# Row maxima over 1024 keys in pairs of PSUM banks in place of twice 512 in single banks

## What is computed

```python
qkv = x @ qkv_w.T + qkv_b                       # reshaped to 16 heads, hd = 8
scores = jnp.einsum('hbds,hbdt->hbst', q, k) / jnp.sqrt(jnp.float32(hd))
w = jax.nn.softmax(scores, axis=-1)             # over 1024 keys
attn = jnp.einsum('hbst,hbdt->hbsd', w, v)
return attn @ out_w.T + out_b
```

## Time and profile before

| | us |
|---|---|
| runs of the kernel | 629.66, 629.94, 626.11 |
| median | 629.66 |
| span of the profiled execution | 623.5 |
| that execution's own time | not shown |
| TensorE busy in the span | 546.7 |
| VectorE busy | 480.4 |
| ScalarE busy | 349.4 |
| mean granted TensorE clock, share of full speed | 0.929 |

### The profile page before, as it was taken

One profiled execution on the slowest core, in us unless ns is written; L12 is line 12 of the kernel. 1 busy time (PEld: TensorE's weight loads), 2 busy tenths in 40 slices (PEclk: granted clock), 3 DMA queues, 4 the chain that ended last, 5 costly groups with the idle time before them and its releaser, 6 DMA issues.

```text
span 623.5 us, 9634 instructions
## 1 busy us (share of the span) xinstructions
PE 546.7 (88%) x2831; PEld 218.8 (35%) x2831; DVE 480.4 (77%) x965; ACT 349.4 (56%) x667; POOL 113.0 (18%) x155
## 2 busy tenths in 40 slices
PE   2986899872591699999999999899999999999887
PEld 2443656561110133333333333233333333323366
DVE  6999579971593388888898898788888888863473
ACT  2764314433000377777777677677777777778551
POOL 6947708334000000100100100100100000000000
PEclk9997899887555599999999999999999999999999
DMA  8030000021221000010010010010010000000001
GB/s 205 8 69 0 2 1 1 5 82 74 87 85 81 25 1 2 27 52 2 29 51 2 29 51 2 32 51 2 19 61 2 2 2 1 1 2 1 1 18 52
DMA packets 14664, 18.95 MB, mean 30 GB/s; under 512 B 3801, under 2 KB 12936, under 8 KB 13448
## 3 DMA queue, kind: packets, MB, share of 16 engines
q1 hardware_dynamic: 13818, 17.54, 8.2%
q0 software_dynamic: 240, 0.46, 0.7%
q10 hardware_dynamic: 550, 0.27, 0.1%
HBM read 12.75 MB, written 4.19 MB: 27 GB/s over the span
## 4 chain that ended last, share of the span: by engine, by line
PE 69%; DVE 16%; DMA 8%; ACT 3%; issue 2%; SPq 2%; POOL 0%; ACTq 0%; DVEq 0%
PE ps L1256 20%; PE ps L1229 18%; PE ps L1294 17%; PE ps L1034 5%; PE ps L1044 5%; DVE mx L895 3%; DMA qt<-nm_s 3%; DVE acc L794 3%; DMA kt<-k_scr 2%; DVE h L710 2%; DVE acc L840 1%; DMA k_scr<-gate 1%; PE ps L1243 1%; ACT gate L648 1%; DVE st L687 1%
## 5 line engine op out<-in xcount | busy, mean ns | idle before, releaser
L895 DVE TENSOR_REDUCE mx<-ps 128x1 f32<-128x512 f32 x512 | 319.5, 681 | 70.8 <-PE ps L1229 70.8
L648 ACT ACTIVATE gate<-ps 128x512 f32<-128x512 f32 x256 | 134.3, 604 | 112.2 <-PE ps L1294 112.2
L1229 PE MATMUL ps<-kt,qt 72*128 72x512 bf16 x384 | 157.7, 417 | 18.0 <-DMA kt<-k_scr 18.0
L1294 PE MATMUL ps<-qt,kt 96*128 96x512 bf16 x384 | 143.0, 386 | 21.6 <-DMA qt<-nm_s 18.2
L648 ACT ACTIVATE acc<-ps 128x512 f32<-128x512 f32 x256 | 132.3, 602 | 49.8 <-PE ps L1294 49.8
L1229 PEld LDWEIGHTS ps<-kt,qt 72*128 72x128 bf16 x384 | 38.3, 100 | 131.9 <-DVE mx L895 81.0
L1256 PE MATMUL ps<-gate,v 128*32 128x512 f32 x512 | 69.3, 611 | 0.7 <-ACT o_sb L639 0.7
L1256 PE MATMUL ps<-acc,v 128*32 128x512 f32 x512 | 68.2, 605 | 0.6 <-ACT acc L648 0.6
L446 POOL CAST nm_s<-nm 16x128 bf16<-16x128 f32 x16 | 4.6, 287 | 331.4 <-DVE nm L908 331.4
L1294 PEld LDWEIGHTS ps<-qt,kt 96*128 96x128 bf16 x384 | 37.5, 99 | 65.0 <-DMA qt<-nm_s 18.8
L1229 PE MATMUL ps<-val 72*128 72x512 bf16 x128 | 48.8, 382 | 0.0
(11 more groups left out here) (181 smaller groups left out, 473.3 us busy)
## 6 DMA issues: line engine op xcount, KB each, us to landing
qt<-q_scr SPq DMA_DIRECT2D x18, 192.0 KB
kt<-k_scr SPq DMA_DIRECT2D x18, 192.0 KB
val<-q_scr SPq DMA_DIRECT2D x6, 192.0 KB
val<-k_scr SPq DMA_DIRECT2D x6, 192.0 KB
x<-in_L_attn_a_x SPq DMA_DIRECT2D x4, 256.0 KB, 4.5
us<-h SPq DMA_DIRECT2D x8, 128.0 KB, 2.4
out<-x SPq DMA_DIRECT2D x4, 256.0 KB, 2.2
q_scr<-attn SPq DMA_DIRECT2D x6, 128.0 KB
```

The lines of the kernel that those rows point to most:

```text
L648: act.activation(pexp[s % NPB][:, j, :], bank(exp_bank(n0, s * QH + j, last)[0]), ACT.Exp, scale=SCALE).then_inc(exp_done, 1)
L895: dve.tensor_reduce(mx[:, half, u // 2, u % 2:u % 2 + 1], bank(MBANKS[k % 4]), AX.X, ALU.max).then_inc(m_read, 1)
L1229: pe.matmul(bank(MBANKS[k % 4]), qt[r][0:QK_ROWS, half, j, c * P:(c + 1) * P], kt[r][0:QK_ROWS, keys, j, :], start=True, stop=True).then_i ...
L1294: pe.matmul(bank(at_bank), keys, qt[r][:, half, j, :], start=True, stop=True).then_inc(exp_mm, 1)
```

## The change

A unit becomes 128 queries x 1024 keys: two matmuls of 512 keys into the two banks of a pair, then one read of 1024 values per row. A half has `NU = 16` units, the lead is `LEAD = 8` of them. The four banks become a ring of `MRING = 2` pairs (`pm`); `turn_max` and `turn_o` take a whole pair and use its first bank. Only the first matmul of a pair waits (`m_free`), only the second signals. `row_max` is gone: a unit's read gives the final maximum, and `turn_max` transposes `mx` itself. The order of a step becomes "emememmev"; `turn_max` stands before unit 2, which is the first m of the steps 5 and 13.

```diff
@@ -54,19 +54,18 @@
 
 
 
-ORDER = "emememevm"
+ORDER = "emememmev"
 EBANKS = (0, 1, 3)
 E_MORE = 24
-MBANKS = (4, 5, 6, 7)
+MRING = 2
 COPY_O_AFTER = 0
-MS = ORDER.count("m")
+MS = ORDER.count("m") // 2
 HT = QH * TC
-NU = 2 * HT
-LEAD = 16
+NU = HT
+LEAD = 8
 MQ = 2 * (NU + 2)
 M0 = NU + LEAD
-ROW_MAX_AT = 1
-TURN_MAX_AT = 3
+TURN_MAX_AT = 2
 TURN_O_AT = 2
 
 
@@ -83,7 +82,7 @@
         NEGATED.append(M0 + n * MQ + units + outputs + half)
 PROJECT_AT = (11, 12)
 SHIFT = 16 * PARTS
-assert MQ % len(MBANKS) == 0 and M0 % len(MBANKS) == 0 and MS * BT == NU and LEAD % MS == 0
+assert MQ % MRING == 0 and M0 % MRING == 0 and MS * BT == NU and LEAD % MS == 0
 assert STEPS % NPB == 0 and QH * STEPS % len(EBANKS) == 1
 
 
@@ -209,16 +208,20 @@
         qk_s = [b.bitcast(BF16).rearrange("p (w i c) -> p w i c", w=2, i=PARTS) for b in qk_s]
         u_rows = h[:, :, :].rearrange("p i d -> p (i d)").rearrange("p (b l) -> p b l", b=B)
         tap_bufs = [attn_f[:, i * CH:(i + 1) * CH] for i in range(4)]
-        mx = sb("mx", [P, 2, HT, 2])
-        mx_row = sb("mx_row", [P, HT])
+        mx = sb("mx", [P, 2, HT])
         nm = sb("nm", [HT, P])
         nr = sb("nr", [HT, P])
         nm_s = sb("nm_s", [HT, PARTS, P], BF16)
 
-        ps = [ctx.enter_context(nc.psum_tensor(f"ps{i}", [P, CH], F32)) for i in range(8)]
+        ps = [ctx.enter_context(nc.psum_tensor(f"ps{i}", [P, CH], F32)) for i in range(4)]
+        pm = [ctx.enter_context(nc.psum_tensor(f"pm{i}", [P, 2 * CH], F32)) for i in range(MRING)]
 
         def bank(i):
-            return ps[i][:, :]
+            return ps[i][:, :] if i < 4 else pm[(i - 4) // 2][:, (i % 2) * CH:(i % 2 + 1) * CH]
+
+        def m_bank(k, keys=0):
+
+            return pm[k % MRING][:, keys * CH:(keys + 1) * CH]
 
         def tap_buf(j):
 
@@ -259,7 +262,7 @@
         exp_mm, exp_done, pv_mm = sem("exp_mm"), sem("exp_done"), sem("pv_mm")
         o_copied = sem("o_copied")
 
-        m_mm, m_read, rows_ready, max_step = sem("m_mm"), sem("m_read"), sem("rows_ready"), sem("max_step")
+        m_mm, m_read = sem("m_mm"), sem("m_read")
         shift_split = sem("shift_split")
         attn_flat = sem("attn_flat")
         ao_biased, stored = sem("ao_biased"), sem("stored")
@@ -892,27 +895,21 @@
             def unit_max(half, u, i, k):
 
                 dve.wait_ge(m_mm, i + 1)
-                dve.tensor_reduce(mx[:, half, u // 2, u % 2:u % 2 + 1], bank(MBANKS[k % 4]), AX.X,
-                                  ALU.max).then_inc(m_read, 1)
-
-            def row_max(half, i):
-
-                dve.wait_ge(m_read, i)
-                dve.tensor_tensor(mx_row[:, :], mx[:, half, :, 0], mx[:, half, :, 1], ALU.max).then_inc(rows_ready, 1)
+                dve.tensor_reduce(mx[:, half, u:u + 1], pm[k % MRING][:, :], AX.X, ALU.max).then_inc(m_read, 1)
 
             def negate(hn, i, k):
 
                 dve.wait_ge(m_mm, i + 1)
                 if not isinstance(hn, int) or hn >= 1:
                     dve.wait_ge(shift_split, hn)
-                dve.tensor_scalar(nm[:, :], bank(MBANKS[k % 4])[0:HT, 0:P], -1.0, None,
+                dve.tensor_scalar(nm[:, :], m_bank(k)[0:HT, 0:P], -1.0, None,
                                   ALU.mult).then_inc(m_read, 1)
 
             def norm_o(n, half, i, k):
 
                 dve.wait_ge(m_read, i)
                 dve.wait_ge(m_mm, i + 1)
-                o = bank(MBANKS[k % 4]).rearrange("p (c j w) -> p c j w", c=TC, j=QH)
+                o = m_bank(k).rearrange("p (c j w) -> p c j w", c=TC, j=QH)
                 dve.reciprocal(o_rc[:, :, :], o[:, :, :, HD]).then_inc(rc_ready, 1)
                 dve.wait_ge(rc_ready, n * 2 + (half + 1))
                 quad_out = attn[:, n, :, :] if isinstance(n, int) else attn[:, bass.ds(n, 1), :, :].rearrange(
@@ -923,8 +920,6 @@
 
             def maxima(hn, half, u, i, k, exist):
 
-                if u == ROW_MAX_AT:
-                    row_max(1 - half, i - u if exist else i)
                 if u == TURN_MAX_AT:
                     negate(hn - 1, i, k)
                     i, k = i + 1, k + 1
@@ -957,7 +952,7 @@
                 for s in range(STEPS):
                     half = s // BT
                     if s % BT == TURN_O_AT and not (first and half == 0):
-                        norm_o(n if half else n - 1, 1 - half, base + k, k)
+                        norm_o(n if half else n - 1, 1 - half, base + k, 1 if last and half else k)
                         k += 1
                         if last and half:
 
@@ -1219,28 +1214,31 @@
 
             def m_free(i):
 
-                if not isinstance(i, int) or i >= len(MBANKS):
-                    pe.wait_ge(m_read, i - (len(MBANKS) - 1))
-
-            def max_mm(r, half, u, i, k):
-
-                (j, c), keys = divmod(u // 2, TC), u % 2
+                if not isinstance(i, int) or i >= MRING:
+                    pe.wait_ge(m_read, i - (MRING - 1))
+
+            def max_mm(r, half, u, keys, i, k):
+
+                j, c = divmod(u, TC)
+                if keys == 0:
+                    m_free(i)
+                mm = pe.matmul(m_bank(k, keys), qt[r][0:QK_ROWS, half, j, c * P:(c + 1) * P],
+                               kt[r][0:QK_ROWS, keys, j, :], start=True, stop=True)
+                if keys:
+                    mm.then_inc(m_mm, 1)
+
+            def turn_max(half, behind, i, k):
+
+                pe.wait_ge(m_read, i - behind)
                 m_free(i)
-                pe.matmul(bank(MBANKS[k % 4]), qt[r][0:QK_ROWS, half, j, c * P:(c + 1) * P],
-                          kt[r][0:QK_ROWS, keys, j, :], start=True, stop=True).then_inc(m_mm, 1)
-
-            def turn_max(hn, i, k):
-
-                pe.wait_ge(rows_ready, hn + 1)
-                m_free(i)
-                pe.transpose(bank(MBANKS[k % 4])[0:HT, 0:P], mx_row[:, :], ident[:, :]).then_inc(m_mm, 1)
+                pe.transpose(m_bank(k)[0:HT, 0:P], mx[:, half, :], ident[:, :]).then_inc(m_mm, 1)
 
             def turn_o(hn, i, k):
 
                 pe.wait_ge(o_copied, hn + 1)
                 m_free(i)
                 for t in range(TC):
-                    mm = pe.transpose(bank(MBANKS[k % 4])[:, t * P:(t + 1) * P], o_sb[:, t * P:(t + 1) * P],
+                    mm = pe.transpose(m_bank(k)[:, t * P:(t + 1) * P], o_sb[:, t * P:(t + 1) * P],
                                       ident[:, :])
                 mm.then_inc(m_mm, 1)
 
@@ -1277,7 +1275,10 @@
                     if tile == 0:
                         pe.wait_ge(shift_in, (n * 2 + half) * SHIFT + SHIFT)
                     if tile == TURN_O_AT and not (first and half == 0):
-                        turn_o(n * 2 + half - 1, base + k, k)
+
+                        if last and half:
+                            pe.wait_ge(m_read, base + k)
+                        turn_o(n * 2 + half - 1, base + k, 1 if last and half else k)
                         k += 1
                     if last and s * QH == E_MORE:
                         pe.wait_ge(m_read, base + k)
@@ -1300,16 +1301,17 @@
                             pv(prev, n - 1, STEPS - 1)
                         elif kind == "m":
 
-                            h, u = divmod(NU + LEAD + s * MS + ORDER[:at].count("m"), NU)
-                            if u == TURN_MAX_AT and not (last and h > 2):
-                                turn_max(n * 2 + h - 1, base + k, k)
+                            pair, keys = divmod(ORDER[:at].count("m"), 2)
+                            h, u = divmod(NU + LEAD + s * MS + pair, NU)
+                            if u == TURN_MAX_AT and not keys and not (last and h > 2):
+                                turn_max((h - 1) % 2, 0 if last and h == 2 else u, base + k, k)
                                 k += 1
                             if last and h >= 2:
                                 continue
-                            if h == 2 and u == 0:
+                            if h == 2 and u == 0 and not keys:
                                 pe.wait_ge(qk_in[nxt], loads(n0 + 1, trip))
-                            max_mm(nxt if h >= 2 else r, h % 2, u, base + k, k)
-                            k += 1
+                            max_mm(nxt if h >= 2 else r, h % 2, u, keys, base + k, k)
+                            k += keys
 
             pe.wait_ge(turned, TURN_QKV + NCH)
             pe.wait_ge(wide_read, WIDE_QK + 2 * NCH)
@@ -1318,9 +1320,10 @@
             k = 0
             for u in range(NU + LEAD):
                 if u == NU + TURN_MAX_AT:
-                    turn_max(0, k, k)
+                    turn_max(0, TURN_MAX_AT, k, k)
                     k += 1
-                max_mm(0, u // NU, u % NU, k, k)
+                for keys in range(2):
+                    max_mm(0, u // NU, u % NU, keys, k, k)
                 k += 1
             quad(0, 0, True, False)
             with pe.Fori(0, 2) as i:
```

## The result

The kernel before: 627.36 us (median of 17 runs, 625.10 to 630.09). The changed kernel: 632.72 us (17 runs, 628.98 to 633.99). Ratio 1.0077, 95% interval 1.0060 to 1.0094: slower by 0.8%, some 4.8 us by this ratio; the two medians lie 5.4 us apart. The forecast was +4.7 us (0.7%), counted from the median of three runs.

A forecast was written before the change was run, and what follows sets the result against it. The prediction took TensorE's queue, not VectorE, to bound every step with maximum matmuls. Its terms, 4.3 for `turn_max`, 0.7 for `turn_o` and -0.3 at the loop edge, gave +4.7: 629.66 becomes 634.4 us, range 629.0 to 638.5.

The forecast's parts named there:

- What bounds the kernel: Steps with maximum matmuls: TensorE's queue bounds them at 2.85 us; VectorE's 15 us less work gains 0 us.
- The second pair's weight loads: Plain steps: loads of m2a would be seen waiting, but without a TensorE gap; margin 0.23 us, stall 0.
- The length of a pair read: VectorE's reads of 1024 values: 1.22 us long, 1.14 from start to start, estimated from `negate` and the old read.
- the bounds from L790 and L794: Range for a read's growth from 512 to 1024 values: 0.41 us by L790, 0.735 by L794; 0.54 taken.
- the Trainium skill's formula: Fixed cost of 120 cycles, 0.125 us, per VectorE read from PSUM; would save 32 us of VectorE time instead of 15.
- The opening: Before the steady steps: 24 pair reads replace 48, first negation perhaps 0.1 to 0.4 us earlier, gaining nothing.
- the cover that the prediction had named: In the opening, the shift's data landing behind the loads of two quads hides an earlier negation, otherwise worth 0.4 us.
- The turn steps: Steps with `turn_max`: m1a could start at 1.35, slot free at 1.66; stall 0.31 us, 14 times, 4.3 us.
- is met two reads earlier: In `turn_max`: the wait for the old half's reads replaces the one for `row_max` and is met sooner.
- The `turn_o` steps: After four transposes the next maximum matmul waits 0 to 0.1 us for its slot; 14 x 0.05 = 0.7 us.
- ScalarE starts its exps 0.23 us earlier: In a step: exps start 1.48 us after the value product against 1.71, so a stall of 0.3 keeps ScalarE fed.
- The loop's edge: At the loop's second round: VectorE resumes 0.5 us earlier, TensorE's 2.07 wait stays; -0.3 us, bounds -0.6 and +0.3.

The follow-up runs named there:

- experiment 5: The kernel before with each read of 512 values cut to 256, half of the keys left out of the maximum: 628.30 us, ratio 0.9984.
- experiment 4: The changed kernel with each pair read taking only its first bank, half of the keys left out of the maximum: 626.41 us, ratio 0.9973.
- experiments numbered 3 and 4: Both on the changed kernel: 3 with order eemmemmev, 629.61 us, ratio 1.0017; 4 with reads of only the first bank, 626.41 us, ratio 0.9973.
- the first experiment: The kernel before with its ring of four single banks and reads of 512, but the changed kernel's order emememmev: 632.26 us, ratio 1.0074.

## Why the prediction was right, and where it was not

**What bounds the kernel.** Right. Plain steps stayed at 2.84 to 2.85 us in every kernel, but for the one step at half clock in the opening of two profiles, with VectorE's load down by 15 us (the change), 106 (experiment 5) or 129 (experiment 4). The second pair's weight loads, which I had expected to see waiting, don't: the 15 waits between 225 and 398 are those of the steps with `turn_max` and `turn_o`.

**The length of a pair read.** Forecast 1.22 and 1.14 from start to start, measured 1.22 and 1.14. The estimate from `negate` and the old read, two readers of PSUM of different width, hit; the bounds from L790 and L794 were not needed. Of the Trainium skill's formula (VectorE: DVE Perf Modes, section on the TRN2 errata) the single instruction is near: an estimate of 1.19 us by it against 1.22. Its fixed 0.125 us per instruction isn't what a run of reads saves: from start to start the rows save 2 x 0.60 - 1.14 = 0.06.

**The opening.** The prediction had the first negation 0.1 to 0.4 us earlier; it came 0.47 later, at 184.29 against 183.82. It had counted 18 pair reads at 1.14. They took 21.18 us:

```profile
163.19 21.18 DVE L898 TENSOR_REDUCE mx<-pm 128x1 f32<-128x1024 f32 x18 [16.24 <-PE pm L1225]
```

They start 1.14 and 1.21 us apart in turn, 1.18 on average, almost as far as two of the old reads (1.20): TensorE waits for a slot there and refills it late. It cost nothing only because the shift's data landed behind the loads at 208.3 as before, the cover that the prediction had named. The first score matmul came at 208.35 (208.38 before).

**The turn steps.** Slot free at 1.66 forecast, 1.65 measured; stall 0.31 forecast, 0.30 seen in the timeline and 0.33 in the step; 14 x 0.31 = 4.3 forecast, 4.57 measured. The extra 0.02 per step is in the step's other spacings and I did not follow it further. The experiments numbered 3 and 4 moved the two sides of this wait separately, and the step time followed both within 0.01 us. What the prediction missed is that the old ring in the new order would have stalled nearly as long, at `row_max`. I had written that the wait for `row_max` "is met two reads earlier"; in the changed kernel that is so, but it kept me from seeing that the order takes the value product's cover away from `row_max` as well.

**The `turn_o` steps.** The sum was near (0.7 forecast for 14, 0.37 measured for 12), the step behind it false. There is no wait for the slot: in the changed kernel the weight load comes 1.65 us after the value product and its matmul at 1.71, just 0.22 behind the score matmul, as it streams. The 0.04 us come from the transposes, which now follow the value product directly and take 0.49 instead of 0.44 until the next score matmul. All kernels with the value product last have it, with either ring (3.32 to 3.33).

**A gain without a price.** I noted that ScalarE starts its exps 0.23 us earlier and used it only as cover. It is also a gain: the value product in the steps with `copy_o` waited for that copy for 0.03 us in the loop and 0.09 outside it (it started 0.14 us after the copy's end each time), and no longer does (0.27 to 0.33 after it): -0.5 us in the looped kernel, -1.2 unrolled.

**The loop's edge.** The term that failed. I gave it -0.3 us, bounds -0.6 and +0.3, from VectorE's earlier restart. The changed kernel's profile lost 2.8 there. I had costed the edge by its idle time alone, though the earlier trace rows stand behind an idle TensorE, and the opening of the same profile shows the granted clock at 0.50 from 208 to 217, behind 18.25 us of idle. In the looped kernels the three intervals took 11.02, 11.08, 11.44, 11.49, 12.70, 12.91 and 14.28 us. The long ones are the changed kernel, the first experiment and the fifth, hence both rings and both orders; the short ones too. The three longest are the three whose profile has the granted clock at 0.50 there, the four others have it at 1.00 throughout. So a good part of it comes and goes with the execution. The part that the prediction did cost was not far off: where the clock stayed up, the new order took 11.08 and 11.02 against 11.49, and 11.44 in the one with the longest idle stretch (2.36). What the sum lacked was a term for the clock.

**What stays open.** Whether the change makes the loss at the edge more frequent. Writing out the loop gained 0.5% in the kernel before and 0.8% in the changed one. The difference, 1.6 us, would say yes; the intervals of the ratios allow for some 2 us, so it isn't shown. The runs one by one lean the same way: 15 of the 17 of the changed kernel took 632.3 to 634.0 us, at least 3.3 above its fastest, and 6 of the 17 of the kernel before lie 3 us or more above its fastest. But where in an execution the time went is on record for the profiled ones alone. Either way most of the cost is accounted for: +3.2 us in steps with the loop written out, 4.4 with the loop's code but without the edge's own row, 4.8 measured by the ratio and 5.4 by the medians.

**The baseline.** The median of three runs, 629.66, was 2.3 us above that of 17. The forecast of 634.4 was 1.7 above the measured 632.72 for that reason. The prediction also put 6.2 us around the span; it is 2.0, and the profile was of a fast execution. The step from before to after was right within 0.1 us by the ratio and within 0.7 by the medians. The first is luck: the missed gains and the small remainders cancel against the turn steps and the edge.

## What to carry to other kernels

Before relieving an engine, take the distance between starts on the one that issues without gaps: if it is the sum of its own spacings, the relief is worth nothing, whatever the waits' totals say. Fewer and larger buffers keep the same bytes but come free later, and here it was the irregular users of the ring, one transpose in eight steps, that paid for it. When an order written by hand is changed, ask of each dependent pair what used to stand between them; moving the consumer 0.22 us later, behind work that was due anyway, took two thirds of the stall away here.

## What was not expected of the hardware

An idle stretch of TensorE of 1.95 to 2.36 us at a loop's second round was followed by the granted clock at 0.50 in some executions and by none of it in others, with a cost between 0 and some 3 us. The length of the idle stretch doesn't tell which: the clock fell behind 1.95, 1.99 and 2.00 us, and stayed up behind 1.96, 2.01, 2.07 and 2.36. Written out, the same work had neither in five profiles, and the median fell by 3 us in the kernel before.

A weight load that begins late cost nothing here as long as its matmul would not have started yet. In the `turn_o` step of the changed kernel the load began only 0.06 us before its matmul, and the matmul kept its distance of 0.22:

```profile
289.11 0.38 PE L1295 MATMUL ps<-qt,kt 96*128 96x512 bf16 x1
289.27 0.10 PEld L1225 LDWEIGHTS pm<-val 72*128 72x128 bf16 x1 [0.17 <-DVE mx L898]
289.33 0.38 PE L1225 MATMUL pm<-val 72*128 72x512 bf16 x1
```

The load's own row is 0.10 us long, which I had taken as the least distance. The row of a load and the start of its matmul may overlap; in the turn step above both start at 227.31.
